# Moving the attention masks from TensorE to GpSimd and VectorE, with a reordered opening

## The reference, cut to what matters

```
attn   = tanh(x @ W1 + b1)                  # [128, 128]
scores = attn @ v                           # [128]
mask   = by the batch's type: l <= j, l >= j, or l != j
p      = softmax(where(mask, scores[None, :], -1e30))   # row j over columns l
x      = x + (p @ x) / count(mask row)      # first layer
out    = x + x @ W[cat] + b[cat]            # second layer: one of 64 matrices
```

## Time and profile before

| | before |
|---|---|
| time, median of 3 runs | 323.19 us (321.76 to 323.30) |
| profiled execution: its time / its span | 322.09 / 320.3 us |
| mean granted TensorE clock | 0.994 of full speed |
| busy of the span: PE, DVE, ACT, POOL | 97%, 89%, 86%, 1% |
| DMA: mean rate | 317 GB/s |
| x tile of 1,024 KB on SP's queue, issue to landing, median | 7.1 us (512 KB: 5.2 us) |
| W of 1,024 KB on SP's queue, issue to landing, median | 8.3 us |

### The profile page before, as it was taken

One profiled execution on the slowest core, in us unless ns is written; L12 is line 12 of the kernel. 1 busy time (PEld: TensorE's weight loads), 2 busy tenths in 40 slices (PEclk: granted clock), 3 DMA queues, 4 the chain that ended last, 5 costly groups with the idle time before them and its releaser, 6 DMA issues.

```text
span 320.3 us, 4751 instructions
## 1 busy us (share of the span) xinstructions
PE 311.7 (97%) x1374; PEld 242.3 (76%) x1374; DVE 283.8 (89%) x300; ACT 274.4 (86%) x447; POOL 3.6 (1%) x17
## 2 busy tenths in 40 slices
PE   8999897999999999999999999999999999999996
PEld 4445675878888887887888788888878888787884
DVE  3558799999999999999999999999999999999950
ACT  2376988979989899998989999898998989899852
POOL 3010000000000000000000000000000000000000
PEclk9999997999999999999999999999999999999999
DMA  7999999899989989998999999898899989974123
GB/s 227 429 356 422 421 382 335 303 354 308 356 308 345 353 300 381 303 376 299 358 322 320 351 328 368 313 350 317 307 405 297 360 311 353 334 282 178 37 96 131
DMA packets 21290, 101.49 MB, mean 317 GB/s; under 512 B 2385, under 2 KB 2386, under 8 KB 11282
## 3 DMA queue, kind: packets, MB, share of 16 engines
q1 hardware_dynamic: 20882, 100.15, 85.2%
q10 hardware_dynamic: 288, 0.79, 0.7%
q0 software_dynamic: 96, 0.26, 0.3%
HBM read 84.41 MB, written 16.78 MB: 316 GB/s over the span
## 4 chain that ended last, share of the span: by engine, by line
PE 91%; ACT 3%; DVE 2%; DMA 2%; issue 1%; SPq 0%; DVEq 0%; ACTq 0%
PE ps_y L564 17%; PE ps_y L565 16%; PE ps_y L566 16%; PE ps_pre L520 11%; PE ps_y L579 4%; PE ps_y L552 4%; PE ps_y L576 4%; PE ps_y L577 4%; PE ps_y L578 4%; PE ps_pre L509 2%; PE ps_pT L543 2%; DMA x_raw<-in_x 2%; PE ps_scores L530 1%; DVE w_lo L378 1%; PE ps_scores L532 1%; ACT w_hi L261 1%
## 5 line engine op out<-in xcount | busy, mean ns | idle before, releaser
L378 DVE TENSOR_TENSOR w_lo<-w_raw,w_hi 128x2048 fp32r<-128x2048 f32 x60 | 137.1, 2285 | 4.0 <-ACT w_hi L261 4.0
L261 ACT ACTIVATE w_hi<-w_raw 128x2048 fp32r<-128x2048 f32 x60 | 115.9, 1933 | 1.5 <-DVE w_raw L366 1.5
L564 PE MATMUL ps_y<-w_hi,xT_hi 128*128 128x512 f32 x240 | 96.6, 403 | 0.3 <-DVE w_lo L378 0.3
L566 PE MATMUL ps_y<-w_hi,xT_lo 128*128 128x512 f32 x240 | 94.4, 394 | 0.0
L565 PE MATMUL ps_y<-w_lo,xT_hi 128*128 128x512 f32 x240 | 94.4, 393 | 0.0
L566 PEld LDWEIGHTS ps_y<-w_hi,xT_lo 128*128 128x128 f32 x240 | 45.3, 189 | 10.0
L564 PEld LDWEIGHTS ps_y<-w_hi,xT_hi 128*128 128x128 f32 x240 | 45.4, 189 | 9.6 <-ACT out_sb L303 0.5
L565 PEld LDWEIGHTS ps_y<-w_lo,xT_hi 128*128 128x128 f32 x240 | 45.4, 189 | 9.3
L405 DVE TENSOR_TENSOR z_lo<-ps_y,z_hi 128x512 fp32r<-128x512 f32 x64 | 43.5, 682 | 6.3 <-ACT z_hi L297 6.3
L297 ACT ACTIVATE z_hi<-ps_y 128x512 fp32r<-128x512 f32 x64 | 39.0, 610 | 9.3 <-PE ps_y L566 4.8
L366 DVE TENSOR_TENSOR w_raw<-w_raw,ident 128x512 f32<-128x512 f32 x63 | 42.8, 681 | 0.6 <-DMA w_raw<-in_L_cond_W 0.6
(11 more groups left out here) (71 smaller groups left out, 284.5 us busy)
## 6 DMA issues: line engine op xcount, KB each, us to landing
w_raw<-in_L_cond_W SPq DMA_DIRECT2D x63, 1024.0 KB, 8.3
out<-out_sb SPq DMA_DIRECT2D x64, 256.0 KB, 5.4
x_raw<-in_x SPq DMA_DIRECT2D x15, 1024.0 KB, 7.1
w_raw<-in_L_cond_W SPq DMA_DIRECT2D x2, 512.0 KB, 6.6
x_raw<-in_x ACTq DMA_DIRECT2D x1, 512.0 KB, 5.9
x_raw<-in_x SPq DMA_DIRECT2D x1, 512.0 KB, 5.2
w_pack<-in_W_b_v ACTq DMA_DIRECT2D x1, 257.0 KB, 3.2
b_raw<-in_L_cond_b POOLq DMA_DIRECT2D x2, 128.0 KB, 7.2
```

The source lines that it names most:

```text
L261: nc.scalar.activation(w_hi[k % NH][:], w_raw[k % NW][:], ACT.Copy).then_inc(w_hi_ready, 1)
L378: nc.vector.tensor_tensor(w_lo[k % NL][:], w_raw[k % NW][:], w_hi[k % NH][:].bitcast(F32), ALU.subtract).then_inc(w_lo_ready, 1)
L564: nc.tensor.matmul(y[:], xT_hi[q][:, c, xs], w_hi[k % NH][:, c, :], start=(c == 0), stop=False)
L566: last = nc.tensor.matmul(y[:], xT_lo[q][:, c, xs], w_hi[k % NH][:, c, :], start=False, stop=(c == DC - 1))
```

## The change

What it does:

- PE's four penalty products per group and its register loads are gone. GpSimd copies the patterns of each group's four batches to a bf16 tile `mask`, two groups ahead (`mask_group`).
- `max_group` becomes four `tensor_tensor_reduce` of 128x128, each of which adds the mask to the scores, negates, writes the result back into the PSUM bank and gives the row minimum (which is -max) as a second output. The exp takes scale -1.
- The product of row sum and count moves from DVE to GpSimd; DVE keeps the reciprocal.
- x of group 0 and the first W come whole: x by SP, W by ACT's queue behind the ids and W1. The bias moves from GpSimd's queue to SP's, behind W of batch 4.
- The hand-written order of ACT and DVE in the opening changes (batches 4 to 9), and their loops start at k = 7. Nothing is reordered inside the loops.

The diff, cut to its core:

```diff
-            sp.dma_start(ids_row[:], ids.rearrange("(a n) -> a n", a=1)).then_inc(ids_in, 16)
-            sp.dma_start(x_raw[0][:, halves[0], :], xg[0][:, halves[0], :]).then_inc(x0_in[0], 16)
+            load_x(0)
             sp.wait_ge(ids_in, 16)
-            cat_0 = sp.value_load(ids_row[0:1, 0:1], min_val=0, max_val=C - 1)
-            for h, c in enumerate(halves):
-                sp.dma_start(w_raw[0][:, c, :], w[bass.ds(cat_0, 1), :, c, :].rearrange("a p c h -> p (a c) h"))\
-                    .then_inc(w0_in[h], 16)
...
             load_w(4)
+            sp.dma_start(b_raw[0:C, :], bias).then_inc(b_low_in, 16)
+            sp.dma_start(b_raw[C:P, :], bias).then_inc(b_high_in, 16)
...
+            def mask_group(g):
+                if g >= 2:
+                    pool.wait_ge(neg_max_ready, g - 1)
+                for i in range(G):
+                    kind = pool.value_load(type_row[0:1, G * g + i:G * g + i + 1], min_val=0, max_val=2)
+                    last = nc.gpsimd.tensor_copy(mask[g % 2][:, i:i + 1, :], penalty[:, bass.ds(kind, 1), :])
+                last.then_inc(mask_ready, 1)
...
-            pool.wait_ge(w_in[2], 16)
-            pool.dma_start(b_raw[0:C, :], bias).then_inc(b_low_in, 16)
-            pool.dma_start(b_raw[C:P, :], bias).then_inc(b_high_in, 16)
+            pool.wait_ge(consts_ready, 7)
+            pool.wait_ge(kinds_ready, 1)
+            mask_group(0)
+            mask_group(1)
+            pool.wait_ge(seen_ready, 1)
+            for g in range(GROUPS):
+                pool.wait_ge(exp_ready, g + 1)
+                if g >= 1:
+                    pool.wait_ge(scale_ready, g)
+                nc.gpsimd.tensor_tensor(row_div[:], row_sum[:], seen[:, G * g:G * (g + 1)], ALU.mult)\
+                    .then_inc(div_ready, 1)
+                if g + 2 < GROUPS:
+                    mask_group(g + 2)
...
                     act.wait_ge(probsT_done, g)
                 for i in range(G):
                     last = nc.scalar.activation(probs[:, i, :], ps_scores[:, i * S:(i + 1) * S], ACT.Exp,
-                                                bias=neg_max[:, i:i + 1], accum_out=row_sum[:, i:i + 1])
+                                                bias=neg_max[:, i:i + 1], scale=-1.0, accum_out=row_sum[:, i:i + 1])
...
+            act.dma_start(ids_row[:], ids.rearrange("(a n) -> a n", a=1)).then_inc(ids_in, 16)
             act.dma_start(w1_pack[:], w1).then_inc(w1_in, 16)
-            act.dma_start(x_raw[0][:, halves[1], :], xg[0][:, halves[1], :]).then_inc(x0_in[1], 16)
+            act.wait_ge(ids_in, 16)
+            cat_0 = act.value_load(ids_row[0:1, 0:1], min_val=0, max_val=C - 1)
+            act.dma_start(w_raw[0][:], w[bass.ds(cat_0, 1)].rearrange("a p c h -> p (a c) h")).then_inc(w_in[0], 16)
...
+            split_w_hi(4)
             tanh_group(1)
-            split_w_hi(4)
-            split_z_hi(3)
             split_w_hi(5)
             exp_group(1)
+            split_z_hi(3)
             copy_out(0)
             scale_group(1)
-            copy_out(1)
             split_xT_hi(2)
             split_w_hi(6)
+            split_z_hi(4)
+            split_mix_hi(1)
+            copy_out(1)
             split_w_hi(7)
-
-            for k in range(G + 1, B + 3):
+            copy_out(2)
+            split_z_hi(5)
+            tanh_group(2)
+            split_w_hi(8)
+            copy_out(3)
+            split_w_hi(9)
+
+            for k in range(G + 3, B + 3):
...
 
             def max_group(g):
                 dve.wait_ge(scores_done, g + 1)
-                nc.vector.tensor_reduce(neg_max[:], ps_scores[:].rearrange("p (b l) -> p b l", b=G),
-                                        AXIS_X, ALU.max, negate=True).then_inc(neg_max_ready, 1)
+                dve.wait_ge(mask_ready, g + 1)
+                for i in range(G):
+                    cell = ps_scores[:, i * S:(i + 1) * S]
+                    last = nc.vector.tensor_tensor_reduce(cell, cell, mask[g % 2][:, i, :], -1.0, 3e38, ALU.add, ALU.min,
+                                                          accum_out=neg_max[:, i:i + 1])
+                last.then_inc(neg_max_ready, 1)
 
             def row_scale_group(g):
-                dve.wait_ge(exp_ready, g + 1)
-                nc.vector.tensor_tensor(row_div[:], row_sum[:], seen[:, G * g:G * (g + 1)], ALU.mult)\
-                    .then_inc(div_ready, 1)
                 dve.wait_ge(div_ready, g + 1)
                 nc.vector.reciprocal(row_scale[:], row_div[:]).then_inc(scale_ready, 1)
...
-            add_identity_0(0)
-            add_identity_0(1)
...
-            split_av_lo(0)
...
+            add_identity(0)
+            split_av_lo(0)
...
                 .then_inc(bias_ready, 1)
+            split_w_lo(4)
             split_av_lo(1)
             add_identity(5)
-            split_w_lo(4)
             max_group(1)
+            split_w_lo(5)
+            row_scale_group(1)
             split_z_lo(2)
             split_z_lo(3)
-            row_scale_group(1)
-            split_w_lo(5)
...
+            split_av_lo(2)
             add_identity(9)
-
-            for k in range(G + 2, B + 1):
+            split_z_lo(5)
+            split_w_lo(8)
+            add_identity(10)
+
+            for k in range(G + 3, B + 1):
...
-                    pe.wait_ge(x_in[g], 16)
+                pe.wait_ge(x_in[g], 16)
...
-            def scores_group(g, kinds):
+            def scores_group(g):
...
                 nc.tensor.matmul(ps_scores[:], ones[:], av_hi[:], start=True, stop=False)
                 pe.wait_ge(av_lo_ready, g + 1)
-                nc.tensor.matmul(ps_scores[:], ones[:], av_lo[:], start=False, stop=False)
-                for i in range(G):
-                    last = nc.tensor.matmul(
-                        ps_scores[:, i * S:(i + 1) * S], ident_bf[:],
-                        penalty[:, bass.ds(kinds[i], 1), :].rearrange("p a l -> p (a l)"),
-                        start=False, stop=(i == G - 1))
-                last.then_inc(scores_done, 1)
+                nc.tensor.matmul(ps_scores[:], ones[:], av_lo[:], start=False, stop=True).then_inc(scores_done, 1)
...
-            warm_up(11)
+            warm_up(7)
...
-                if k < B and g + 1 < GROUPS:
-                    if b == 0:
-                        kinds = [load_kind(G * (g + 1))]
-                    elif b == 1:
-                        kinds += [load_kind(G * (g + 1) + i) for i in (1, 2)]
-                    elif b == 2:
-                        kinds += [load_kind(G * (g + 1) + 3)]
```

45 lines of the change are left out of this document (12 added, 33 removed).

## The result

| | before | after |
|---|---|---|
| time, median (range, runs of one comparison) | 322.48 us (320.54 to 323.30, 4) | 328.73 us (328.26 to 329.84, 4) |
| ratio, 95% interval | | 1.021 (1.018 to 1.024): slower |
| span of the profiled execution | 320.3 us | 326.2 us |
| row maximum of group 3 / 15, start | 71.67 / 296.73 | 73.00 / 302.99 |
| one round of four batches | 18.755 us | 19.166 us |

The starts and rounds are those of the one profiled execution of each kernel.

A forecast was written before the change was run, and what follows sets the result against it. Bound: the ring in which VectorE and ScalarE wait for each other once per round, TensorE nearly as long. Opening -1.0, ring +8.2, end -0.1 make +7.1 on 322.9: 330.0 us, range 322.5 to 337.

The forecast's parts named there:

- The ring: Loop: VectorE and ScalarE wait for each other once per round, setting 18.755 us; TensorE's fall to 18.40 gives nothing there.
- TensorE's play: Loop: without penalty products TensorE stands about 1.0 us a round, most of it at av_lo's product.
- The pieces: Row maximum in four: exp starts 1.35 after first piece, 0.63 later than now; 13 x 0.63 = +8.2 us (4.0 to 17.3).
- The tail of 0.42: Row maximum: last piece's results reach ScalarE about 0.26 + 0.16 us after that piece starts.
- My own low end: Row maximum: pieces of 0.20 plus a read of 0.04; exp 1.03 after the first piece, 0.31 later than now.
- The opening: Before the loop: transfer delay of 1.0 to 1.5 us hidden, fewer TensorE stands and no lower clock; -1.0 us (0 to -2).
- My walk through the orders: Opening: stepping through ScalarE's and VectorE's new orders puts xT_lo of group 2 at 38.7, against 38.63 now.
- The end: Behind the last scores: penalties gone save 0.31 once, TensorE waits some 0.2 for exp and transposes; net -0.1 us.
- GpSimd: nothing that can be told, as costed: Loop: row product and mask copies on GpSimd cost nothing directly; a late row product up to 0.3 a group.
- the rival: Loop: GpSimd's SBUF reads stop VectorE, each by its own 0.29 (row product 0.15); 335 to 347 us, chance 0.14.
- The clock: Loop: TensorE's clock falls every round from its standing, some 0.6 x 13 on top; 338 us, chance 0.04.

The follow-up runs named there:

- masks alone: Kernel before with only masks and row product on GpSimd, four maximum pieces, no penalty products; old opening except bias on SP's queue: 326.05 us, 1.013 of before.
- the copy ahead of the exp: ScalarE's output copy at b = 3 moved before the exp, at b = 0 behind xT_hi; on masks alone, against that kernel's 326.05 us: 316.68 us, 0.986 of before.
- halves with 11 warm-up products: Changed kernel with x of group 0 and first W in halves and 11 warm-up products instead of 7, as before: 326.38 us, 1.015 of before.
- the two kernels before with moved copies: Kernel before with ScalarE's output copies moved: behind the roundings 321.56 us (0.999); ahead of the exp at b = 3, behind xT_hi at b = 0, 321.15 us (0.996).
- the run with halves and 7 warm-up products: Changed kernel with x of group 0 and first W in halves as before, keeping 7 warm-up products: 327.93 us, 1.017 of before.

## Why the prediction came out as it did

The forecast was 330.0 (322.5 to 337), slower; measured were 328.73 and slower. By span, +7.1 was forecast and +5.9 came. Its steps:

- **The ring sets the pace in the loop: right.** The round is the old one plus what stands between maximum and exp, to 0.01 us, and giving back the single reduction gives back the old round. TensorE's play of 0.8 a round (19.17 - 18.37) stayed play; the forecast looked for most of it at av_lo, where it stood 0.4 a round (5.3 in 13 times).
- **The pieces: right mechanism, wrong size.** Forecast were 3 x 0.31 + 0.42 = 1.35 from first piece to exp; measured 0.71 + 0.42 = 1.13. The tail of 0.42, put together from two small rows, was exact. The pitch was not: 0.21 for the first piece and 0.25 for the others, where the line through two three-operand rows (0.26) plus a guessed 0.05 for the read gave 0.31. My own low end, 0.20 + 0.04 = 0.24, was the nearer one. The accumulator read has no place of its own in the row: it starts at the same moment as the next piece. The pieces that start with a read beside them take 0.04 longer than the first; whether that is the price of the read stays open. So 13 x 0.41 = 5.3 instead of 8.2; 2.9 too much, and the rounds of 19.17 lie under the 19.3 to 19.5 that were to show the forecast right.
- **The Trainium skill's price of small pieces.** "VectorE: DVE Perf Modes", section "The TRN2 errata — SBUF-src ops pay a fixed extra latency per instruction", gave an estimate of 0.29 a piece, from its formula for a two-tensor operation. The trace agrees as to the duration of the first piece (0.29; the others take 0.33). What the engine pays is the pitch, 0.21 and then 0.25, and that is less.
- **The opening: wrong.** -1.0 was forecast, all of it from the penalties that TensorE no longer has, and nothing for the edits of transfers and order; at group 3, less one ring step of 0.41, +0.92 came. Of the 0.83 that the round from group 2 to 3 was to give, 0.60 came (19.40 is 0.23 over the loop's rounds, 19.58 was 0.83 over them); the loss lies ahead of group 2, whose maximum is 1.51 late. The gain was there (-1.59 with the penalties alone gone, -1.40 with the masks in their place), but the edits cost 0.90 + 1.83 = 2.73. What fell is the sentence that the late first W is hidden behind ScalarE's rounding of W of batch 4: its products started 2.20 later (12.20 against 10.00) and not 1.0 to 1.5, the first maximum was 1.94 later than with halves and a full warm-up, and 1.83 of it was still there at group 3. My walk through the orders had xT_lo of group 2 at 38.7; it came at 40.52. The idle time that I thought the new order closes is still there (0.78 before that xT_lo). I had the third row maximum near 51.9 (53.60) and the first product near 7.9 (6.43): the delay was not in x but in W.
- **The end:** -0.36 instead of -0.1.
- **GpSimd: nothing that can be told, as costed.** The row product was in time, and without the copies the rounds were the same. The rule of "SBUF — State Buffer", section "Who interferes with whom", in the Trainium skill was the rival's ground. The trace agrees with it as to who waits: of copies of 0.29 those that meet the identity or w_lo take 0.56 and, as a pair, 2.68. It also shows the other direction, on VectorE and then GpSimd:

```profile
231.29 2.42 DVE L394 TENSOR_TENSOR w_lo<-w_raw,w_hi 128x2048 fp32r<-128x2048 f32 x1 [0.43 <-ACT w_hi L271]
...
235.23 2.29 DVE L387 TENSOR_TENSOR xT_lo<-x_raw,xT_hi 128x2048 fp32r<-128x2048 f32 x1 [0.31 <-ACT xT_hi L265]
```
```profile
231.28 0.29 POOL L222 COPY mask<-penalty 128x128 bf16 x1 [0.36 <-issue]
```

The copy began 0.01 ahead of w_lo, and w_lo took 2.42 instead of 2.29. The rule speaks of the whole length of the first; here that would be 0.28, and 0.13 was measured. That 0.13 went out of the wait before xT_lo (0.31 instead of 0.44). The price that I gave this rival, each copy's full length on VectorE, was wrong by its direction: of the 51 w_lo in the loop two took 2.42 and the others 2.28 to 2.29, so it is nearly always GpSimd that is held up. Most of VectorE's operations follow each other without a gap, which fits.
- **The clock: nothing in the loop, something ahead of it.** It reads 1.00 from 80 to 100 us and from 100 to 180 us, in spite of the gaps. The one fall is where the round from group 2 to 3 is 0.23 longer than the others (window from 60 to 80 us, columns as above):

```profile
60.00:80.00 20.00, 19.78 (x82) 16.24 (x83) 18.97 (x25) 18.05 (x31) 4.53 (x7) 0.92 0.90 328
```

From 60 to 62 us the granted clock is 0.50 of full speed, the lower of TensorE's two levels (1.2 GHz); just ahead TensorE had stood 0.83 and 1.52 us. In the kernel before it stood 1.16 and 1.41, and the clock fell there. All fourteen traces agree on the price: in the seven with such a fall between 49 and 65 us (before, after, masks alone with and without the copy ahead of the exp, halves with 11 warm-up products, and the two kernels before with moved copies) the round from group 2 to 3 is 0.23 to 2.41 longer than the loop's, and in the seven without it that round is the loop's to 0.02. Whether the clock falls is not decided by the stands alone: without penalties TensorE stood 1.19 and 1.41, in the run with halves and 7 warm-up products 0.86 and 1.53, and in neither trace did it fall. So part of each difference at group 3 is the clock of the one execution that was profiled.

So the forecast was near for a mixed reason: 2.9 too much for the pieces, 1.9 too little for the opening, 0.3 too much for the end. The mechanism of the loop was right; that errors of opposite sign left only 1.2 us of the span was luck.

## What to carry to other kernels

When two engines wait for each other once per round, write the ring down as a sum of pitches: an edit is worth what it changes on that sum and nothing else, until the next engine's own round is reached. Here taking 0.30 a round from the busiest engine gave nothing in the loop (the 0.7% of that run came from the first rounds and the end), and moving ScalarE's copies off the ring gave 0.4% alone. The two together gave 1.4%, even with 0.41 of new work on the ring. And look for the work on the ring that nobody there waits for: it belongs into the gap in which that engine waits.

## What was not expected of the hardware

- An operation with an accumulator output on VectorE costs hardly more than its main part: 0.25 from piece to piece at 128x128 (0.21 for the first), with a 0.14 read that runs beside the next piece.
- GpSimd's copy of 128x128 bf16 takes 0.29 alone and up to 2.45 beside w_lo; VectorE's 51 w_lo in the loop took 2.28 to 2.42 us (median 2.29), so the most that one of them lost is 0.14.
- TensorE's first eight products show at which of its two clock levels it runs where the profile does not. The granted clock reads 1.00 over the first 20 us in every run, but the trace's own list of clock levels begins only with a rise to full speed: at 5.28 us in the changed kernel, at 11.18 in the run with halves and 7 warm-up products. In the latter the products that end ahead of 11.18 take 1,061 ns (the first 1,194) and their weight loads 337; behind it they take 592 and 190, as in the changed kernel from the second product on. All fourteen traces fit. Where the list begins at 4.8 to 6.2 us, ahead of the first product, the eight take 3.67 to 3.70 us; at 6.7 to 7.4, 3.9 to 4.3; at 9.7 to 11.2, 5.4 to 6.0.
- What decides when the clock rises stays open. With 7 warm-up products, which end at 5.5 us, it rose beside the last of them in three traces and 4.2 to 5.7 us behind them in four; with 11, which end at 6.3, it rose at 5.3 to 7.4 in all seven. The slow products were hidden wherever the first W came late anyway.
